# A two-layer graph network: the smallest edge kind multiplied directly, it and the second kind's tables by float32 matmuls on weights as loaded, two of three tiles gathered plainly

## The reference

```python
h = jnp.maximum(_layernorm(x, axis=-1), 0.0)
feat = jnp.concatenate([n_f[edge_src], n_f[edge_dst]], axis=1)      # n_f is h
e_hh = relu(feat[:E_HH] @ W_hh + b_hh)
e_oo = relu(feat[E_HH:E_HH + E_OO] @ W_oo + b_oo)
e_ho = relu(feat[E_HH + E_OO:] @ W_ho + b_ho)
logit = (e_f @ W_a + b_a)[:, 0]
alpha = softmax of logit over the edges that share a dst
z_f = segment_sum(alpha[:, None] * n_f[edge_src], edge_dst)
nf2 = concatenate([n_f, z_f], axis=1)
h_new = relu(nf2[:NH] @ W_hn + b_hn); o_new = relu(nf2[NH:] @ W_on + b_on)   # NH = 128
x = x + concatenate([h_new, o_new])
# then a second layer: layernorm, relu, h @ W.T + b, and a normalized sum over the graph
```

## Time and profile before

| | us |
|---|---|
| median of 3 runs (651.59 to 653.91) | 653.9 |
| the profiled execution, its own time | 651.15 |
| its span, first to last instruction | 649.0 |
| TensorE matmul busy | 556.4 (86%) |
| VectorE busy | 454.9 (70%) |
| ScalarE busy | 307.4 (47%) |
| GpSimd busy | 176.3 (27%) |

### The profile page before, as it was taken

How to read it: one execution, slowest core, us unless ns; L and a number is a source line. 1 busy time by engine, 2 the same in 40 slices (tenths; PEclk the granted TensorE clock), 3 DMA queues, 4 the chain that set the end, 5 groups by cost and what they waited for, 6 DMA issues and landing times.

```text
span 649.0 us, 8205 instructions
## 1 busy us (share of the span) xinstructions
PE 556.4 (86%) x2376; PEld 412.9 (64%) x2377; DVE 454.9 (70%) x958; ACT 307.4 (47%) x485; POOL 176.3 (27%) x165
## 2 busy tenths in 40 slices
PE   0799999999839998959899997558949999779987
PEld 0688777777617776647576775224738778667865
DVE  6715256786985879988989887486795289783252
ACT  2623312214088996556565755399743182322200
POOL 2000300165464664555647642200030000000000
PEclk9999999999968999989889999688968899979999
DMA  8334453499999999999999997943355075121021
GB/s 330 122 135 163 151 202 124 144 259 380 316 308 356 330 343 325 303 321 333 284 361 327 349 348 262 232 136 103 127 213 208 16 249 198 41 88 42 0 82 48
DMA packets 55973, 140.51 MB, mean 216 GB/s; under 512 B 6274, under 2 KB 6402, under 8 KB 55938
## 3 DMA queue, kind: packets, MB, share of 16 engines
q0 software_dynamic: 20624, 74.98, 37.5%
q1 hardware_dynamic: 27072, 50.34, 22.0%
q10 hardware_dynamic: 8242, 14.75, 6.1%
HBM read 123.27 MB, written 16.78 MB: 216 GB/s over the span
## 4 chain that ended last, share of the span: by engine, by line
PE 57%; DVE 20%; DMA 11%; ACT 6%; issue 4%; POOL 1%; ACTq 0%; DVEq 0%; POOLq 0%
PE ps L638 35%; DMA gath<-tab_b,tabl_i 8%; PE ps L624 6%; PE ps L588 5%; DVE gath L893 4%; PE ps L797 3%; ACT onehot L482 3%; PE ps L769 3%; DVE ring_l L868 2%; PE ps L782 2%; DVE gath L888 2%; DMA gath<-tab_a,tabl_i 2%; DVE onehot L910 2%; DVE logit_d L932 1%; DVE logit_d L1021 1%
## 5 line engine op out<-in xcount | busy, mean ns | idle before, releaser
L638 PE MATMUL ps<-ring_h,actT_h 128*128 128x512 f32 x520 | 226.0, 435 | 28.2 <-ACT stage L453 16.4
L638 PE MATMUL ps<-ring_h,actT_l 128*128 128x512 f32 x520 | 206.4, 397 | 0.0
L638 PE MATMUL ps<-ring_l,actT_h 128*128 128x512 f32 x520 | 206.2, 397 | 0.0
L435 ACT CAST ring_h<-raw 128x512 fp32r<-128x512 f32 x176 | 105.0, 616 | 118.4 <-PE ps L638 82.8
L482 ACT ACTIVATE onehot<-onehot,lgs 128x512 bf16<-128x512 bf16 x192 | 124.6, 712 | 69.4 <-DVE onehot L910 55.3
L868 DVE TENSOR_TENSOR ring_l<-raw,ring_h 128x512 fp32r<-128x512 f32 x176 | 116.8, 685 | 43.2 <-ACT ring_h L435 42.9
L638 PEld LDWEIGHTS ps<-ring_h,actT_h 128*128 128x128 f32 x520 | 99.9, 192 | 60.8 <-ACT stage L453 18.3
L638 PEld LDWEIGHTS ps<-ring_h,actT_l 128*128 128x128 f32 x520 | 99.7, 192 | 22.4
L638 PEld LDWEIGHTS ps<-ring_l,actT_h 128*128 128x128 f32 x520 | 100.0, 192 | 20.3
L293 POOL DMA_INDIRECT gath<-tab_a,tabl_i x64 | 71.0, 1109 | 150.2 <-DVE gath L893 77.0
L588 PE MATMUL ps<-onehot 128*128 128x512 bf16 x292 | 83.8, 397 | 20.8 <-ACT onehot L482 17.8
(11 more groups left out here) (162 smaller groups left out, 505.1 us busy)
## 6 DMA issues: line engine op xcount, KB each, us to landing
raw<-in_L_gnn_W_ho_dram SPq DMA_DIRECT2D x32, 256.0 KB
raw<-in_L_gnn_W_oo_dram SPq DMA_DIRECT2D x32, 256.0 KB
raw<-in_L_gnn_W_hh_dram SPq DMA_DIRECT2D x32, 256.0 KB
raw<-in_L_gnn_W_on_dram SPq DMA_DIRECT2D x32, 256.0 KB
raw<-in_L_gnn_W_hn_dram SPq DMA_DIRECT2D x32, 256.0 KB
tab_a<-stage ACTq DMA_DIRECT2D x24, 256.0 KB
tab_b<-stage ACTq DMA_DIRECT2D x24, 256.0 KB
raw<-in_L_gnn_W_dram SPq DMA_DIRECT2D x16, 256.0 KB
```

The costliest lines, as they stand in the source:

```text
L435: nc.scalar.copy(ring_h[:, k, :], raw[:, k % RAW, :]).then_inc(s_high, 1)
L638: mm = nc.tensor.matmul(ps[:, first + m, :], w, v, start=(k == 0 and i == 0), stop=(k == KT - 1 and i == 2))
```

## The change

1. The kinds' order is ho (chunks 0 to 3), hh (4 to 7), oo (8 to 11).
2. hh has no tables. The normalized rows `h` are stored to device memory (`h_d`), the two hh tiles' source and destination rows are gathered from it and transposed by TensorE (`hh_transposes`, in chunk 0), and the result `featT` is multiplied by W_hh directly (`hh_chunk`, 16 matmuls in each of the four chunks). The logits come from PSUM (`hh_edges`).
3. In chunks 4 to 11 the matmuls are float32, on the weight pieces as loaded (`raw`): no `round_w`, no `low_w`, one matmul where there were three. In the oo chunks the other operand is `actT`, the two parts of h put together again (8 VectorE additions); it lies over `hrow`, which is reloaded in chunk 12.
4. Of tiles 0 to 61, those with q % 3 not 0 are plain (41 of 62; it was 31 of 62).
5. The places of counts, edges, sums and seeds are all new. The weights' loads of chunks 5 to 12 wait for TensorE (`s_slot`) where they waited for `low_w`. In the node chunks weights are rounded 6 steps ahead (2 before).

```diff
-        PLAIN = [q for q in range(T_HO + T_OO) if q % 2]
+        PLAIN = [q for q in range(T_HO + T_OO) if q % 3]
...
+            for m in range(NM):
+                sp.wait_ge(s_h, m + 1)
+                sp.dma_start(h_d[m * P:(m + 1) * P, :], hrow[:, m, :]).then_inc(s_hd, 16)
...
+            for i in range(2 * T_HH):
+                pool.indirect_dma_start(out=gath[:, NM + i, :], out_offset=None, in_=h_d[:, :],
+                                        in_offset=bass.IndirectOffsetOnAxis(ap=hh_i[:, i:i + 1], axis=0)).then_inc(s_hg[i], 16)
...
+        EDGES_AT = {(5, 2 * i): (i,) for i in range(4)}
+        EDGES_AT |= {(c, k): (4 + 6 * (c - 6) + i,) for c in (6, 7) for i, k in enumerate((0, 1, 3, 4, 6, 7))}
+        EDGES_AT |= {(c, k): tuple(16 + 12 * (c - 8) + k + k // 2 + i for i in range(1 + k % 2)) for c in (8, 9) for k in range(KT)}
+        EDGES_AT |= {(10, k): (40 + k,) for k in range(KT)} | {(11, 2 * i): (48 + i,) for i in range(4)}
+        EDGES_AT |= {(13, 4): (52,), (13, 7): (53,), (14, 3): (54,), (14, 6): (55,), (15, 0): (56,), (15, 2): (57,), (15, 4): (58,)}
+        LAST_EDGES = (59, 60, 61)
...
+        SUMS_AT = {(8, 4): HH_TILES[:1], (8, 5): HH_TILES[1:]}
+        SUMS_AT |= {(9, k): (2 * k - 2, 2 * k - 1) for k in range(1, KT)}
+        SUMS_AT |= {(10, k): (14 + 2 * k, 15 + 2 * k) for k in range(KT)}
+        SUMS_AT |= {(11, k): (28 + 2 * k, 29 + 2 * k) for k in range(1, KT)}
+        SUMS_AT |= {(12, k): (44 + k,) for k in range(KT)}
...
+            def hh_chunk(n, half):
+                q = CH_HH + 2 * n + half
+                for k in range(KT):
+                    pe.wait_ge(s_raw[k], 16 * q + 16)
+                    f = half * KT + k
+                    for t in range(T_HH):
+                        b = NM + 2 * n + t
...
+                        mm = nc.tensor.matmul(ps[:, b, :], featT[:, f, t * P:(t + 1) * P], raw[:, k, :], start=(f == 0), stop=(f == 2 * KT - 1))
...
+            def oo_chunk(q):
...
+                        if k == 0:
+                            pe.wait_ge(s_copied, i * NM + m + 1)
+                            if q == CH_OO:
+                                pe.wait_ge(s_hhd, m + 1)
+                        mm = nc.tensor.matmul(ps[:, NM + m, :], actT[:, k, m * P:(m + 1) * P], raw[:, k, :], start=(k == 0), stop=(k == KT - 1))
...
+            def hh_edges(n):
+                dve.wait_ge(s_bias, 48)
+                for t in range(T_HH):
...
+                    step(nc.vector.tensor_tensor(ps[:, b, :], ps[:, b, :], bias2[:, 0, c], ALU.add))
+                    nc.vector.scalar_tensor_tensor(out=ps[:, b, :], in0=ps[:, b, :], scalar=0.0, in1=wa_b[:, c],
+                                                   op0=ALU.max, op1=ALU.mult, accum_out=lgh[:, t, n:n + 1]).then_inc(s_hhd, 1)
```

More of the change, by code:

```diff
@@ L332, in _ @@
             bias(0, b_hh)
[L333 to L335 removed]
+            for q in range(FIRST, TG):
+                if q == T_HO:
+                    for p in range(T_HO - LAG, T_HO):
+                        if p not in PLAIN:
+                            gather_add(p, 1)
+                    tables_landed(2)
                 gather_src(q, kinds_of(q))
@@ L625, in product, with chunk @@
                 return mm
-            def chunk(q, first, ms, bank_free=None, before=None, after=None, counted=False):
+            def chunk(q, first, ms, bank_free=None, before=None, after=None, counted=False, nth=None):
                 for k in range(KT):
@@ L646, in edge_chunk @@
             def edge_chunk(q, before=None, after=None):
-                chunk(q, NM, range(NM), lambda m: pe.wait_ge(s_copied, q * NM + m + 1), before, after, counted=True)
+                chunk(q, NM, range(NM), lambda m: pe.wait_ge(s_copied, q * NM + m + 1), before, after, counted=True, nth=q)
             reg = [None]
@@ new lines, in oo_chunk @@
+            def oo_chunk(q):
+                i = TABLES.index(q)
+                for k in range(KT):
+                    sums(SUMS_AT.get((q, k), ()))
+                    pe.wait_ge(s_raw[k], 16 * q + 16)
+                    for m in range(NM):
+                        if k == 0:
[3 more added lines that the diff above has]
+                        mm = nc.tensor.matmul(ps[:, NM + m, :], actT[:, k, m * P:(m + 1) * P], raw[:, k, :], start=(k == 0), stop=(k == KT - 1))
+                        if k == KT - 1 and m < NM - 1:
+                            mm.then_inc(s_bank, 1)
+                    mm.then_inc(s_slot, 1)
@@ new lines, in add_logits, with sums @@
+            def add_logits(q, place, s, order):
+                pe.wait_ge(s_part, order + 1)
+                accumulate(reg[0], place, s, 3)
+            def sums(tiles):
+                for q in tiles:
+                    if q == TG:
+                        pe.wait_ge(s_ccopy, 3)
+                        open_masked(2, 1)
+                    if q == 0:
+                        pe.wait_ge(s_kfree, NM)
+                        open_masked(0, 2)
+                    if q == T_HO:
+                        pe.wait_ge(s_kfree, 2 * NM)
+                        open_masked(1, 3)
+                    if q % TC == 0 or q in (T_HO, TG):
+                        reg[0] = codes(q // TC, TC)
+                    add_logits(q, q % TC, SLOT[q], ORDER[q])
+                    if q in KIND_ENDS:
+                        close_banks(s_kind)
@@ L720, in _ @@
+            for n in range(NN):
+                for half in range(2):
+                    hh_chunk(n, half)
+            pe.wait_ge(s_whole, KT)
+            for q in range(CH_OO, CH_EDGE):
+                oo_chunk(q)
             q = CH_EDGE
-            base = NM + NM * CH_EDGE
-            waits = (NM * CH_EDGE + 1, None, base + 4, None)
+            base = NM + NM * len(TABLES)
+            waits = (base - NM + 1, None, base + 4, None)
             for c, (_, _, _, ms) in enumerate(NODE[0]):
```

418 lines of the change are left out of this document (245 added, 173 removed).

## The result

The changed kernel takes 728.96 us in the median of 4 runs (727.66 to 732.26), the kernel before 653.9 (651.59 to 656.56). The ratio is 1.115, with a 95% interval of 1.111 to 1.119: slower by 11.5%, where no change was forecast, and outside the range. The profiled execution has a span of 726.9 us against 649.0.

A forecast was written before the change was run, and what follows sets the result against it. The DMA engines' gathered rows were taken to set the pace in the middle, TensorE in chunks 10 and 11. 384.5 + 79 + 185.8 = 649.3 against a span of 649.0, so no change: 654 us, range 629 to 670.

The forecast's parts named there:

- Chunks 0 to 3: Transposes move into chunk 0, chunks 1 to 3 take 26.0 us each; chunk 3 ends at 131.5, was 122.6.
- Matmul price: hh and oo chunks: a float32 matmul of 512 columns takes four passes, 0.91 us; the sum on TensorE stays even.
- for the share I take 1.03: Chunks 4 to 9: 166.6 us of DMA work until tile 39 served at share 1.03, 161.7 us; rows there at 300.6.
- The account: DMA work priced from queue shares, checked on the kernel before: tile 51 through at 363.5, trace 364.0; tile 39 309.5 against 314.8.
- The price of the gathers: DMA engines' cost, split from the gather queue's 243.4 us: 2.4 us for an adding gather, 1.5 for a plain one.
- the second rival: Ten late tiles, 52 to 61, before the row maximum: adding gathers land late, 16 us, time 670 us; chance 0.20.
- The sign I gave for being wrong there: Tile 39 much sooner than forecast would mean a dearer adding gather than 2.4 us, or that the waits were for slots.
- Chunks 10 and 11: TensorE bound: 64 float32 matmuls of 58.2 us and 30 sums of 0.66, 78.0 us; chunk 11 ends at 384.5.
- To the row maximum: From chunk 11's end, ten tiles still to gather, DMA work just hidden: 79 us, was 83.4; maximum at 463.5.
- The rest: Behind the row maximum: 185.8 us, unchanged; rounding further ahead is of no use in a stretch that waits for the softmax.
- The first and third rivals: First: rows come in time, 631 us, chance 0.30. Third: float32 at two passes, chunks 10 and 11 68 us, 644 us, chance 0.05.
- the first rival: Chunks 8 and 9: rows come in time, VectorE limits, chunk 10 opens 23.5 us sooner; 626 to 645 us, chance 0.30.

The follow-up runs named there:

- the repaired versions: Changed kernel with every second (or every) tile plain, node weights rounded two steps ahead, h reloaded later, edges spread, `hh_edges` earlier; without or with earlier sums: 661.33 to 666.56 us.

## Why the prediction was wrong

The span was forecast at 649.3 us and is 726.9. Of the 78 us between, 43 are there when chunk 10 opens, the others behind it.

*Chunks 0 to 3: right.* 133.0 against 131.5; chunk 0 with TensorE's 32 transposes took 28.6 us against 28.2.

*Matmul price: right in kind, 6% high.* Each float32 matmul of 512 columns is two records, and eight records (four matmuls) take 3.43 us in the changed kernel's chain:

```profile
413.92 3.43 PE ps L806 x8
```

That is 0.858 us a matmul, against 0.91. By the Trainium skill's four passes (FP8 and Floating Point Precision, TensorE Precision Notes) and 0.228 us for a pass the estimate was 0.91 as well. The trace has 0.43 us a record, 1.9 times a split matmul's 0.228, which agrees with four passes within 6%. And the run on 128 columns shows that for oo it did not matter; the float32 chunks 4 to 7 ended when forecast.

*The step that failed: "for the share I take 1.03".* I took the saturated DMA engines of the kernel before as the thing that sets the pace of the rows, and carried the saturation over to a different plan of gathers. The account fitted tile 51 within 1 us, and the fit persuaded me; but a full resource says only that it is not slower than the rest, not how far below it the next limit stands. The change lowered the work of the DMA engines (to 4.0 us a tile, 161.7 for 40) and at the same time made the loop of slots three tiles long instead of four, from about 3.6 to about 4.8 us a tile. That lifted the loop above the DMA engines. Measured: 5.1 us a tile at a share of 0.86, and tile 39 43 us late. The first sum of chunk 10, forecast for 306.5, is as late:

```profile
350.00 1.46 PE L671 MATMUL ps<-onehot 128*128 128x512 bf16 x3 [4.34 <-ACT onehot L549]
```

The price of the gathers was not the fault. In the packet records of the trace before, most of the 4 KB packets of the gathers take 159 ns, and 4060 take 300 to 350 ns, about as many as the adding gathers have (33 times 128). In the kernel before with all tiles plain, 380 are left of that second group. For 128 rows over 16 engines this makes 1.3 and 2.6 us, an estimate; I had 1.5 and 2.4. I had written down the pieces of the loop in the second rival (a slot is refilled only once VectorE has released it; an adding gather is issued two tiles later) and applied them only to the last ten tiles, not to the 52 ahead. The sign I gave for being wrong there ("the waits were for slots") was the right one; it should have been a rival with a price.

*Chunks 10 and 11: 78.0 us forecast, 91.6 measured* (from the first sum at 350.0 to the last matmul at 441.6). In the stretch of chunk 10 TensorE is busy all the time (39.6 us), as forecast; 3 us more lie in its first sums, ahead of that stretch. Chunk 11 took 11 us more than the 38 reckoned. 6 of them are the rounding six steps ahead, which I had called of no use and so priced at nothing; the other 5 were not tried. In all that step costs 13 us, because the engine that runs ahead is an in-order queue and what it waits for depends on TensorE.

*To the row maximum: 79 forecast, 99.2 measured.* Chunk 12 took 34.7 us and not 22, by the same wait (24.1 with the rounding two steps ahead). The ten tiles' gathers were issued from 457.3 on, 15 us behind the chunk instead of 6.5: chunk 11's stores start only at 445.2, behind a rounding on ScalarE that waits for its piece. With the rounding two steps ahead the gathers start 7 us behind the chunk. The first of their edges ran at 483.7, and the second rival's direction was right, though late issue and VectorE's queue did it: no gather's landing is in the chain of this stretch. The two-step version brings the stretch to 88.6 us, so the rounding is 11 of the 20 us; how the other 9 divide was not tried.

*The rest: right,* 185.8 us both times.

*The first and third rivals* (faster) were wrong. The granted clock fell to 0.70 and 0.81 in chunks 8 and 9, where TensorE mostly waited; in chunk 10, where it counts, it was 0.97. What it cost in all is not separated from the waits. A slip of the range: its lower end, 629, is not the middle of the first rival's 626 to 645, which is 635.5.

What stays open: the last 1% between the repaired versions and the kernel before. Chunk 3 ends 10 us later in all of them, which is of that size, but no run takes it away.

## What to carry to other kernels

When slots, an in-order issuing queue and a long landing are in one ring, write down for each issue which slot it takes over and whose release that is; if it leads back to the landing before, a tile takes (landing + work) divided by the tiles in one turn, and as long as the long landing stays in the ring, a change that uses more slots a tile puts fewer tiles in a turn. A resource at 100% in the profile gives a floor for the change and not yet its forecast: price the limits that stand below it, and price them anew for the plan that comes. And an engine that works ahead in an in-order queue holds back all that is behind it for as long as its input is not free to load.

## What the runs showed that I had not expected

Cutting the oo matmuls to a quarter of their columns saved 4 us of 729, with the clock in chunk 9 down from 0.81 to 0.67. Issuing the adding gather one tile behind instead of two gained 25 us on one kernel and lost 12.6 on the other. And an adding gather takes 6.8 to 10.9 us from issue to landing in the changed kernel (median 8.1) while a plain destination gather takes 3.8 to 9.4 (median 5.5):

```profile
DMA to landing us min/median/max: 6.8/8.1/10.9
```
